# A graph and feed-forward kernel: GpSimd's weight split two tiles later, weights turned behind two units, fewer pair adds in the edge stage

## The reference, cut to what matters

```python
x = x + L0_gnn(layernorm(x), src, dst, ...)     # messages of 20000 edges, summed by source node
x = x + L0_ffn(layernorm(x), ...)               # each row goes through one of 64 experts
# L1_gnn: 4 blocks of
y = cond_layer_norm(x, cond, ...)
y = sparse_attention(y, src, dst, wq, wk, wv, wo, ...)   # attention over the edges
x = x + y
y = cond_layer_norm(x, cond, ...)
x = x + relu(y @ m_w1 + m_b1) @ m_w2 + m_b2
# L1_ffn: weights quantized to -1, 0, 1 times a scale per group of 128
h = silu(y @ gate.T) * (y @ up.T)
x = x + h @ down.T
```

## Time and profile before

| | |
|---|---|
| median of three runs | 3019.26 us |
| the profiled execution, whole / span | 3022.77 us / 3021.0 us |
| TensorE busy | 2551.6 us, 84% |
| VectorE busy | 1880.1 us, 62% |
| ScalarE busy | 1365.9 us, 45% |
| GpSimd busy | 1187.2 us, 39% |
| mean granted TensorE clock | 0.927 of full |

### The profile page before, as it was taken

One profiled execution on the slowest core, in us unless ns is written; L12 is line 12 of the kernel. 1 busy time (PEld: TensorE's weight loads), 2 busy tenths in 40 slices (PEclk: granted clock), 3 DMA queues, 4 the chain that ended last, 5 costly groups with the idle time before them and its releaser, 6 DMA issues. The chain is left out here.

```text
span 3021.0 us, 38863 instructions
## 1 busy us (share of the span) xinstructions
PE 2551.6 (84%) x13585; PEld 2188.0 (72%) x13585; DVE 1880.1 (62%) x3536; ACT 1365.9 (45%) x2725; POOL 1187.2 (39%) x918
## 2 busy tenths in 40 slices
PE   3999999735867078997998998989989989988999
PEld 3787777534646067896786886878868878876997
DVE  2888888562563345676745776546767467766862
ACT  1555565421244143664434664435644356644431
POOL 2888888784632201225102224012242022362420
PEclk9999999767878579999999999999999999999999
DMA  7434344217639711101112101211011121121101
GB/s 244 91 77 80 71 81 78 23 9 225 187 96 292 207 38 51 34 17 52 60 40 61 42 27 42 82 52 34 18 52 59 41 62 40 33 68 42 53 22 34
DMA packets 172004, 220.42 MB, mean 73 GB/s; under 512 B 111710, under 2 KB 120345, under 8 KB 164384
## 3 DMA queue, kind: packets, MB, share of 16 engines
q1 hardware_dynamic: 80253, 170.59, 19.4%
q0 software_dynamic: 91552, 47.27, 7.8%
HBM read 177.10 MB, written 40.15 MB: 72 GB/s over the span
## 5 line engine op out<-in xcount | busy, mean ns | idle before, releaser
L2104 POOL TENSOR_SCALAR prob<-prob,rden,linked 125x1250 f32<-125x1250 f32 x160 | 223.5, 1397 | 923.7 <-DVE rden L2071 923.7
L579 POOL DMA_INDIRECT pairs<-late_cnt,late_idx x160 | 361.8, 2261 | 109.7 <-DMA pairs<-late_cnt,late_idx 55.9
L2022 ACT CAST prob_high<-ps 125x375 fp32r<-125x375 f32 (+1 forms) x480 | 230.9, 503 | 266.8 <-PE ps L1984 266.4
L2063 DVE CUSTOM_DVE_ANT_0 prob<-ps,mask 125x1250 f32<-125x1250 f32 x160 | 233.1, 1457 | 127.7 <-PE ps L1960 109.2
L2076 DVE TENSOR_TENSOR prob_low<-ps,prob_high 125x375 fp32r<-125x375 f32 (+1 forms) x480 | 270.0, 585 | 46.6 <-ACT prob_high L2022 46.5
L538 PE MATMUL ps<-onehot,mhi 125*128 125x512 f32 (+1 forms) x960 | 254.8, 375 | 19.0 <-DVE onehot L426 18.9
L1973 PE MATMUL ps<-ident,prob 125*125 125x125 f32 x1600 | 252.4, 273 | 17.3 <-POOL prob L2104 10.7
L338 POOL DMA_INDIRECT Hg<-h_rows,dsti x160 | 223.4, 1396 | 103.3 <-issue 98.2
L1973 PEld LDWEIGHTS ps<-ident,prob 125*125 125x125 f32 x1600 | 232.3, 187 | 29.7 <-POOL prob L2104 22.9
L538 PE MATMUL ps<-onehot,mlo 125*128 125x512 f32 (+1 forms) x960 | 244.5, 364 | 0.0
L2014 ACT ACTIVATE prob<-prob,top 125x1250 f32<-125x1250 f32 x160 | 214.7, 1342 | 44.4 <-DVE top L2063 35.4
(11 more groups left out here) (408 smaller groups left out, 6110.4 us busy)
## 6 DMA issues: line engine op xcount, KB each, us to landing
mask<-mask_d SPq DMA_DIRECT2D x40, 546.9 KB
sg_wd<-L_ffn_Wd SPq DMA_DIRECT2D x32, 512.0 KB, 6.8
w_ring<-L_ffn_Wd SPq DMA_DIRECT2D x16, 1024.0 KB
w_ring<-L_ffn_Wu SPq DMA_DIRECT2D x16, 1024.0 KB
pairs<-zeros POOLq DMA_DIRECT2D x18, 625.0 KB, 25.5
keyrow<-keys_d SPq DMA_DIRECT2D x40, 244.1 KB
kept<-g_d SPq DMA_DIRECT2D x40, 224.0 KB
g_d<-kept SPq DMA_DIRECT2D x30, 224.0 KB
```

The costliest lines, as they stand in the source:

```text
L579: nc.gpsimd.indirect_dma_start(pairs[a][:, :], bass.IndirectOffsetOnAxis(T.E.late_idx[:, c:c + 1], 0), T.E.late_cnt[:, c:c + 1], None, com ...
L2022: s.copy(M.pt[0][:, n % 3, 0:w], T.ps[0:P, 3 + n % 4, 0:w]).then_inc(high, 1)
L2063: v.tensor_tensor_reduce(M.prob[:, r, :], S(u)[0:P, 0:N], M.mask[:, it % MASKS, :], 1.0, 3.0e38, ALU.add, ALU.min, M.top[:, r:r + 1]).then ...
L2104: nc.gpsimd.tensor_scalar(M.prob[:, r, :], M.prob[:, r, :], M.rden[:, r:r + 1], T.linked[:, it:it + 1], ALU.mult, ALU.mult).then_inc(norme ...
```

## The change

Three edits. In the row stages, GpSimd's `split` and `carry` come two tiles later in its loop (for the row stage behind attention alone). In the feed-forward stage, for j = 0 only, `unit(1)`, `gate(1)` and `sigmoid(1)` come ahead of `turn_w(1)`, `low_w(1)` and `high_w(1)`; and `low_y(9)` comes ahead of `measure(1)`. In the edge stage, 68 pair adds are issued instead of 84: 57 by the end of group 37, then 7 and 4; the stages behind it keep 14, 10 and 10, and `experts` gets 58 instead of 42.

```diff
--- before.py
+++ after.py
@@ -32,7 +32,8 @@
 EG = 4
 NG = ET // EG
 SG = 4
-EARLY_ADDS = 84
+EARLY_ADDS = 68
+PACED_ADDS = 60
 WB, WRING = 2, 4
 DUMMY = N * N
 ZEROING = 16 * (-(-N // 128) + 1)
@@ -345,7 +346,7 @@
                     for g in range(NG):
                         if g + 2 < NG:
                             fetch(g + 2)
-                        more = EARLY_ADDS * (g + 1) // NG
+                        more = PACED_ADDS * (g + 1) // NG if g < NG - 2 else EARLY_ADDS - 4 * (NG - 1 - g)
                         pool.wait_ge(idx_ready, more // EG + 1)
                         pair_adds(pool, nc, T, pairs, n, more)
                         n = more
@@ -1605,11 +1606,11 @@
                             o_lo(t + 1)
                         pool.wait_ge(g_in[t], 32)
                         nc.gpsimd.tensor_tensor(g(t), g(t), bias, ALU.add).then_inc(biased, 1)
-                        if 2 <= t < KD + 2:
-                            split(t - 2)
-                        if t >= 6:
-                            carry(t - 6)
-                    for t in range(NT - 6, NT):
+                        if 4 <= t < KD + 4:
+                            split(t - 4)
+                        if t >= 8:
+                            carry(t - 8)
+                    for t in range(NT - 8, NT):
                         carry(t)
                 else:
                     for k in range(KD):
@@ -2333,16 +2334,19 @@
                 scales(NT - 1)
                 low_y(NT - 3)
                 low_y(NT - 2)
+                low_y(NT - 1)
                 measure(1)
-                low_y(NT - 1)
                 choose(1)
                 for j in range(KF):
                     gate(NS * j)
+                    if j == 0:
+                        gate(1)
                     if j + 1 < KF:
                         low_w(j + 1)
                     if j + 2 < KF:
                         measure(j + 2)
-                    gate(NS * j + 1)
+                    if j > 0:
+                        gate(NS * j + 1)
                     if j + 2 < KF:
                         choose(j + 2)
                     if j == KF - 1:
@@ -2413,9 +2417,11 @@
                     unit(NS * j)
                     if j == 0:
                         turn_y(NT - 1)
+                        unit(1)
                     if j + 1 < KF:
                         turn_w(j + 1)
-                    unit(NS * j + 1)
+                    if j > 0:
+                        unit(NS * j + 1)
                     unit(NS * j + 2)
                 for t in range(NT):
                     down(t)
@@ -2480,9 +2486,12 @@
                 scale(1)
                 for j in range(KF):
                     sigmoid(NS * j)
+                    if j == 0:
+                        sigmoid(1)
                     if j + 1 < KF:
                         high_w(j + 1)
-                    sigmoid(NS * j + 1)
+                    if j > 0:
+                        sigmoid(NS * j + 1)
                     if j == KF - 1:
                         high_h(0)
                     sigmoid(NS * j + 2)
```

## The result

The changed kernel takes 2965.23 us, the median of four runs (2961.19 to 2971.33), against 3017.84 us for the kernel before, measured beside it on the same chip (3013.62 to 3020.27). The ratio is 0.9829, with a 95% interval of 0.9808 to 0.985: it is **52.6 us faster**. The forecast was 63.3 us, 2956 us, with a range of 2936 to 2988.

A forecast was written before the change was run, and what follows sets the result against it. Bounds differed by stage: GpSimd in the edge stage, a four-engine ring of waits in the row stages, TensorE in feed-forward. Terms -36.6 + 1 + 9 - 43 + 6.3 = -63.3 us took 3019.3 to 2956 us, range 2936 to 2988.

The forecast's parts named there:

- edge stage, pace and tail: Edge stage: fewer adds take GpSimd off the path, last group 36.6 us earlier; adds behind the last fetch cost +1 us.
- experts stage: Experts stage: 16 added adds delay the mask's chain, so ScalarE waits for the first logarithm's input: +9 us.
- row stages: Four row stages behind attention: later splits end the engines' circular waiting, four periods a stage fall from 6.98 us: -43 us.
- feed-forward: Start of feed-forward: measure(1) behind low_y(9) delays the serial chains of weights 1 and 2: +6.3 us.
- What is late next is TensorE and VectorE at 11.17 us: Edge stage: once GpSimd leaves the path, TensorE and VectorE set 11.17 us a group instead of 12.39.
- Rival 2: Edge stage keeps half its loss, VectorE or a lowered clock holding about 11.8 us: 18 us more, 2974 us; chance 0.10.
- The tail: End of the edge stage: 13 adds instead of 7 behind the last fetch, mostly covered by idle time and room: +1 us.
- The room of 28.5 us: Experts stage: of the mask chain's 37.5 us push only 9 us shows, 28.5 us less than with no room.
- Rival 1: Experts stage: the mask's chain has no room, all 37.5 us reach the stage's end: 28.5 us more, 2984.5 us; chance 0.08.
- The period of 4.3 us: Row stages behind attention: a tile takes 4.3 us instead of 6.98 once GpSimd's split no longer waits for ScalarE.
- Rival 3: Row stages: GpSimd starves VectorE's shift; one stall a stage 2985 us, chance 0.06; three a stage 3044 us, chance 0.02.
- Rival 4: Feed-forward: unit(1) fills TensorE's wait and the chain costs nothing: 7 us less, 2949 us; chance 0.10.

The follow-up runs named there:

- run 5: Changed kernel with no paced pair adds in the edge stage and 8 early adds instead of 68, 60 more in the experts stage: 3094.45 us (one run).
- run 4: Changed kernel with measure(1) put back ahead of low_y(9), unit(1) still ahead of turn_w(1): 2962.21 us, ratio 0.9822.
- run 9: Changed kernel with each group's pair adds issued behind the first of its four fetches instead of the fourth: 2959.66 us, ratio 0.9811.
- run 2: Kernel before with only the splits and carries of the row stages behind attention two tiles later: 2967.07 us, ratio 0.9839.
- run 3: Kernel before with the feed-forward edit alone: 3019.45 us, ratio 1.0019.
- run 8: Kernel before with the splits and carries one tile later instead of two, nothing else: 2965.64 us (one run).
- run 6: Changed kernel with 70 paced adds and 78 in all in the edge stage instead of 60 and 68: 2961.41 us, ratio 0.9816.

## Why the prediction was right, and where it wasn't

The time, 2965.2 us, is 9 us above the forecast. Every term had the right sign, and the misses are of both signs: against the profiled pair the edge and experts stages fell 18.5 us short and the row stages gave 9 us too much, 6 to 7 of them the stall in the base. So some of the closeness is luck.

| term | forecast | profiled pair | alone |
|---|---|---|---|
| edge stage, pace and tail | -35.6 | -21.1 | -24.6 |
| experts stage | +9 | +13.0 | +15.7 |
| row stages | -43 | -52.0 | -46.7 |
| feed-forward | +6.3 | +5.9 | +6.1 |
| together (the untouched stretches give 2.7 back in the pair) | -63.3 | -54.2 | -49.5 |

- **Edge stage: the mechanism was right, the size was off by 14 us.** "What is late next is TensorE and VectorE at 11.17 us" took the pace of the first groups as that of the others. TensorE does need 11.2 us at full clock (run 5: 11.24). The step that failed is that GpSimd leaves the path once it has time to spare. Its adds lengthen VectorE's one-hots, for which TensorE waits: at a clock of 1.00 that is 11.39 us in run 4 against 11.22 in run 9, with the same adds in another phase. Of the other 0.14 us of the 11.53, 0.11 is a busier TensorE, at a granted clock of 0.990. In the kernel before, the adds of the first nine groups had begun 5.4 us into a group at the median, and these groups were nearly free of this; in the changed one they aren't, which the forecast had not thought of: 8 x (11.62 - 11.17) = 3.6 us there, and 30 x (11.53 - 11.17) = 10.8 us behind them. Rival 2 named this outcome, a pace held by VectorE or a lowered clock, and priced it at 18 us; what came is 14, and it is both. The clock was in the base too: of the 12.39 us a group there, TensorE waited 0.63 at a clock of 0.957, so about half of the loss per group wasn't waiting.
- **The tail** was forecast at +1 us; it grew from 20.55 to 22.92 us. But in runs 2, 3 and 8, whose edge stage is that of before, it was 22.50, 20.61 and 22.50 us, so a growth between 0.3 and 2.4 us is all that can be read. That the 13 adds end before the next stage's first, with 4.65 us to spare, was as forecast.
- **Experts stage: the chain's push and its length were both a little short.** The load moved by 40.2 us instead of 37.5; 3.4 us of that is that GpSimd waited 5.58 us for its last add to land, where it had waited 2.19. From load to logarithm I had taken 11.2 + 3 = 14.2 us, and it was 207.78 - 187.99 = 19.8 us: the first `pm_m` load, issued at 880.75 at the latest, let VectorE go on only at 896.44, 15.7 us later. So the logarithm came 16.9 us late instead of 9, and the stage 13.0 us. The room of 28.5 us that the forecast implied was measured at 25 to 36 us. Rival 1, no room at all, is out: 16 adds would have cost 37 us.
- **Row stages.** The period of 4.3 us was forecast and is 4.15 to 4.46 us. That makes 4 x 4 x (6.98 - 4.30) = 43 us; 46.7 us were measured alone. The rest is in the eighth tile, whose add waited for TensorE and came 7.9 us behind the seventh in two of the stages and 7.4 in the last, and now comes 6.3 us behind it. The forecast had ended its count at tile 7.
- **The stall** of 7.52 us is in the base of the profiled pair and not in the change. Rival 3, with GpSimd starving the shift, was right in kind: stalls of 2.45 us twice (run 3, whose row stages are those of before), 3.97 (run 6), 3.73 and 3.77 us (run 8) came, each ending within 0.02 us of the end of an unbroken run of GpSimd instructions. Its worst case didn't come: in the eight executions with the splits two tiles later there is one stall over 1.3 us. GpSimd's unbroken run there is up to 14.1 us long in the first three stages, and the other shifts that begin in it last 0.2 to 0.35 us. The place in the run doesn't decide: 8.46 us into it one shift lasted 3.97 us in run 6 and 0.20 to 0.26 us in the other executions, and in the order of before, 9.55 us into it, 7.52 us once and 1.29 to 1.33 us else. What decides stays open. (Its price of 29 us for one a stage counts four, though one of them was in the base already; three more are 22 us.)
- **Feed-forward.** Both chains came as worked out: `turn_w(1)` 5.6 us late (6.05), `turn_w(2)` 4.3 us late (5.2), TensorE's waits 5.20 and 3.46 us (6 and 3.5), the stage 5.9 us longer (6.3). Run 4 shows that the place of `measure(1)` is the cause. Rival 4, that `unit(1)` fills the wait, is out for a reason that the forecast had only half: even with `measure(1)` first the wait moves to weights 2.
- **The rule of the Trainium skill** ("SBUF — State Buffer", "Who interferes with whom") gave the direction again, but not the size: 3.73 us of wait in run 8 is three GpSimd instructions, where by the rule it would be the rest of one, 1.29 us at most. The same section says that a `tensor_scalar` on VectorE can contend with GpSimd when it runs in a mode that uses both ports, and takes descriptor generation to need the write port (it calls this inferred). The one-hot is a `tensor_scalar`; it takes 0.87 us for 1250 columns, 0.70 ns each, where the `tensor_tensor` of 1024 columns (L474) takes 1.21 us, 1.18 ns each. That either it or the DMA instruction beside it is lengthened, and not both, agrees with a port that one of them holds at a time. By the rule it would be blocked to the other's end; here the lengthened one-hots within an add end 0.23 us before the add does.

## What to carry to other kernels

When an engine that issues DMAs stops being the bottleneck, look at what its instructions overlap with on the engine that feeds the next bound: the same adds 3 us earlier in the group were worth about 0.2 us a group at the same clock, and 0.3 with the clock. Work that is moved off one bound lands in the room of another chain; measure that room (here 25 to 36 us) and move no more than fits. Before an instruction is queued behind another on an in-order engine, ask whether the gap in which it used to stand was free.

## What was not expected of the hardware

- A one-hot `tensor_scalar` on VectorE (125 x 1250) takes 0.87 us alone. Beside a GpSimd indirect accumulate it takes 1.12 us on average and up to 1.42, beside an indirect fetch up to 1.30 (kernel before). Where a one-hot begins half a microsecond behind an add, either it takes 1.41 us and the add 2.16, or it takes 0.87 and the add 2.60 (23 and 7 times in the changed kernel). In all executions together 174 one-hots of over 1.25 us lie wholly within an add; each ends 0.22 to 0.23 us before it.
- A VectorE shift of one column, 0.16 us, lasted 2.45 (twice), 3.73, 3.77, 3.97 and 7.52 us, each time until an unbroken run of GpSimd instructions ended; others that began inside such runs, some at the same place in them, lasted 0.2 to 1.4 us.
